# Second expert layer: the second group's scatters and the returns of finished tiles go out in pairs, each pair after the preceding pair has landed

## The reference, cut to what matters

```python
xf = x.reshape(-1, D)
logits = xf @ Wr.T + br
expert_idx = jnp.argmax(logits, axis=-1)               # one expert of 8 per token
h = relu(einsum('td,efd->etf', xf, W1) + b1[:, None, :])
y = einsum('etf,edf->etd', h, W2) + b2[:, None, :]
out = y[expert_idx, arange(tokens)]
x = _layernorm(x + out)
```

## Time and profile before

| what | number |
|---|---|
| runs, median (lowest, highest) | 1368.16 us (1364.99, 1369.56) |
| profiled execution, span | 1397.4 us |
| PE busy in the span | 1272.1 us (91%) |
| DVE busy | 1097.7 us (79%) |
| POOL busy | 1013.4 us (73%) |
| ACT busy | 947.2 us (68%) |
| chain that ended last | PE 49%, ACT 21%, DVE 16%, issue 8%, another core or an unknown queue 2% |
| L2079, 46 returns | 44.8 us busy, 974 ns each on average |
| L1972, 32 scatters of the second layer | 958 ns each (median) |

### The profile page before, as it was taken

The page is one execution under the profiler, slowest core; times in us unless marked ns, Lnnn a source line. Parts: engine busy times, 40 slices in busy tenths (PEclk is TensorE's granted clock), DMA queues, the critical chain, the costliest instruction groups (busy, mean ns, idle before and its releaser), DMA issues.

```text
span 1397.4 us, 27753 instructions
## 1 busy us (share of the span) xinstructions
PE 1272.1 (91%) x9894; PEld 962.1 (69%) x9894; DVE 1097.7 (79%) x1829; ACT 947.2 (68%) x1630; POOL 1013.4 (73%) x620
## 2 busy tenths in 40 slices
PE   6799999999999999999998779999989999986695
PEld 2567767676777676766766646689966666656693
DVE  5799999999999999999999953333357888874475
ACT  5888988898889888988988842245545555532243
POOL 2789999999999999999999916223334665664442
PEclk9999999999999999999999999999999999998798
DMA  5545434543444454444444351312152000021223
GB/s 187 145 131 161 138 139 118 161 149 129 139 139 165 133 150 139 164 132 152 139 146 111 114 216 47 90 44 86 56 157 86 2 1 1 13 64 34 79 72 100
DMA packets 153014, 154.73 MB, mean 111 GB/s; under 512 B 96624, under 2 KB 121712, under 8 KB 143168
## 3 DMA queue, kind: packets, MB, share of 16 engines
q1 hardware_dynamic: 148112, 143.16, 32.8%
q0 software_dynamic: 4768, 9.81, 2.2%
HBM read 138.66 MB, written 20.20 MB: 114 GB/s over the span
## 4 chain that ended last, share of the span: by engine, by line
PE 49%; ACT 21%; DVE 16%; issue 8%; another core or an unknown queue 2%; DMA 2%; POOL 1%; SPq 1%; DVEq 1%; POOLq 0%; ACTq 0%
DVE hh L887 7%; PE pq L410 6%; ACT da L720 6%; PE pa L506 4%; PE py L525 3%; ACT pa L725 3%; PE bank L1562 3%; PE bank L1558 2%; PE pr L2016 2%; PE bank L1572 2%; PE pr L2219 2%; PE pr L2030 2%; PE bank L1478 2%; DVE hh L897 2%
## 5 line engine op out<-in xcount | busy, mean ns | idle before, releaser
L1042 POOL TENSOR_TENSOR hc<-hh,cs 128x1024 f32<-128x1024 f32 x256 | 596.9, 2369 | 24.6 <-DVE hh L887 21.7
L887 DVE TENSOR_TENSOR_SCAN hh<-da,st,pa 128x512 f32<-128x512 f32 x240 | 292.7, 1261 | 14.1 <-PE pa L506 12.6
L525 PE MATMUL py<-ident,hc 128*128 128x128 f32 x2048 | 268.4, 277 | 7.4 <-ACT yt L738 5.8
L525 PEld LDWEIGHTS py<-ident,hc 128*128 128x128 f32 x2048 | 229.1, 141 | 54.4 <-issue 29.1
L506 PEld LDWEIGHTS pa<-dg,dtut 64*128 64x128 f32 x2560 | 160.9, 189 | 107.0 <-issue 103.2
L506 PE MATMUL pa<-dg,dtut 64*128 64x128 f32 x2560 | 189.8, 285 | 29.6 <-DVE hh L887 20.6
L720 ACT ACTIVATE da<-dt,w 128x512 f32<-128x512 f32 x320 | 209.7, 711 | 0.2
L897 DVE TENSOR_TENSOR_SCAN hh<-pa,st,hh 128x512 f32<-128x512 f32 x144 | 175.2, 1265 | 6.1 <-POOL hh L1032 3.7
L725 ACT ACTIVATE pa<-dt,w 128x512 f32<-128x512 f32 x192 | 124.5, 680 | 35.2 <-DVE hh L887 20.8
L410 PE MATMUL pq<-xn,w 128*128 128x512 f32 x248 | 124.6, 627 | 3.6 <-ACT xn L755 3.6
L1032 POOL TENSOR_TENSOR hh<-dtu,bs 128x1024 f32<-128x1024 f32 x48 | 112.8, 2365 | 3.1 <-issue 1.9
(11 more groups left out here) (341 smaller groups left out, 2643.8 us busy)
## 6 DMA issues: line engine op xcount, KB each, us to landing
cs<-bcrows SPq DMA_DIRECT2D x64, 1024.0 KB, 4.9
dg<-blocks SPq DMA_DIRECT2D x80, 256.0 KB, 5.0
bs<-bcrows SPq DMA_DIRECT2D x48, 256.0 KB, 3.7
blocks<-bcrows SPq DMA_DIRECT2D x320, 1.0 KB, 3.2
xsorted<-in_pads SPq DMA_DIRECT2D x13, 387.0 KB, 5.7
rot<-in_rot SPq DMA_DIRECT2D x4, 1024.0 KB, 4.9
wx<-in_l_w SPq DMA_DIRECT2D x4, 1024.0 KB, 10.0
ysort<-ytoken SPq DMA_DIRECT2D x14, 256.0 KB
```

The costliest lines, as they stand in the source:

```text
L525: i = pe.matmul(py[:, h * CH + kt * P:h * CH + (kt + 1) * P], hc[s % HCS][:, h, t], ident[:, :], is_transpose=True, start=n == 0 and kt == ...
L887: v.tensor_tensor_scan(hh[(NS * m + nj) % HHS][:, h, :], da[q % DAS][:, :], inflows, 0.0 if first else st[:, m % 2, nj, h:h + 1], ALU.mult ...
L1042: g.tensor_tensor(hc[s % HCS][:, :, :], hh[s % HHS][:, :, :], cs[j % 2][:, s % CG, :].unsqueeze(1).broadcast_to([P, HF, CH]), ALU.mult).th ...
```

## The change

In place 1's scatters GpSimd waits before every second tile, instead of before tile 8 alone, until all scatters of the place issued so far have landed. In the returns GpSimd waits before the tiles 2, 4, ..., 22 of each place until all returns of that place issued so far have landed. Nothing else differs.

```diff
 def scatter_gpsimd(place, tiles):
     ...
     for i in tiles:
-        if place and i and i % 8 == 0:
+        if place and i and i % 2 == 0:
             g.wait_ge(s_scat1[place], scat0[place] + 16 * i)
 ...
 def return_gpsimd(j):
     if j % SG == 0:
         g.wait_ge(s_token, j // SG + 2)
     g.wait_ge(s_ys, J0 + j + 1)
+    if j % SG and j % SG % 2 == 0:
+        g.wait_ge(s_ret1[j // SG], ret0[j // SG] + 16 * (j % SG))
     g.indirect_dma_start(out=ytoken, ...).then_inc(s_ret1[j // SG], 16)
```

## The result

| | before | after |
|---|---|---|
| runs, median (lowest, highest) | 1368.86 us (1364.99, 1372.72) | 1416.16 us (1415.07, 1417.48) |
| ratio to before, 95% interval | | 1.0346 (1.0320 to 1.0373) |
| profiled execution, span | 1397.4 us, a second one 1364.4 us | 1413.6 us |

The change costs 47.3 us. It was forecast as slower, at 1404 us in a range up to 1411; the direction and the mechanism held, the size did not.

A forecast was written before the change was run, and what follows sets the result against it. VectorE's row of finished tiles bounded the kernel; with the waits GpSimd's steps would. Without the profiled loss the last return moves from 1351.4 to 1387.5 us, and 1368.2 + 36.1 gives 1404 us, range 1374 to 1411.

The forecast's parts named there:

- The baseline: Profiled span without its loss is 1369.1 us, near the runs' 1368.2; the last return before the change starts at 1351.4.
- the 28.3 us: Time lost between tiles 6 and 33 on VectorE in the profiled execution, taken to be absent from the timed runs.
- Rival B: Timed runs have the same 28 us loss, so only 7.8 us are added: 1376 us; chance 0.18.
- C: Unknown releaser is GpSimd's own transfer traffic in every run, and pairs end it: not slower, 1362 us; chance 0.07.
- D: Waits are mostly met already, since tiles come 3.79 us a pair: no change, 1368 us; chance 0.05.
- The mechanism: GpSimd's 61 paced scatter and return steps become the bound; every tile is done before its return's turn.
- the tail: From the start of the last return to the end: 17.7 us, unchanged.
- the late sorted tiles: SyncE's load of place 1's sorted tiles goes from 1291.23 to about 1300 us, costing nothing in the end.
- the hold: VectorE, at about 1323.5 us, waits 24 us for place 0's tokens until 1347.6; tile 45 is finished at about 1374.
- The scatters: Place 1's scatters on GpSimd: 7 of 15 steps are boundaries, putting the last scatter at 1297.6 us, 8.7 us later.
- The price of one wait among the returns: Each of 22 boundaries among GpSimd's returns takes 2.71 us start to start, between 2.23 and 3.15, instead of 1.262.

The follow-up runs named there:

- the scatters alone: Changed kernel with only place 1's scatters in pairs, the returns running free as before: 1378.13 us, ratio 1.0074.
- the first experiment: The kernel before, unedited, profiled a second time: span 1364.4 us; its table sets first scatter, first return, last return and end against the changed kernel.
- returns alone: Changed kernel with only the returns in pairs, the scatters waiting once, at tile 8: 1408.07 us, ratio 1.0288.
- place 0 alone: Changed kernel with only place 0's returns in pairs, scatters as before: 1392.52 us, ratio 1.0163.
- the short load: Changed kernel with the load of place 0's tokens bringing one tile of each piece of four: one run, 1414.24 us.
- the waits turned: Changed kernel with the two waits ahead of a return in the other order, landing first, then finished tile: 1409.73 us, ratio 1.0286.
- two pairs in flight: Kernel before with returns in pairs, each waiting for the pair before the preceding one, a semaphore each for even and odd pairs: 1374.71 us, ratio 1.0047.
- the fours: Changed kernel with scatters as before and returns in fours, each begun once the preceding four has landed: 1388.16 us, ratio 1.0140.

## Why the prediction was wrong, step by step

**The baseline, right.** The step that took the 28.3 us out of the profiled execution put the last return 82.95 us after the first scatter (1351.4 less 1268.45); the second profile has 83.4. Rival B (the loss in every run, 1376 us) is thereby out. So is C: in the second profile GpSimd's transfers follow each other just as closely, and nobody waits for an unknown releaser. D is out by GpSimd's timeline, where it stands idle for 2 us or more ahead of each of the 22 boundaries. The second profiled execution ran like the timed ones, so the 27.8 us named under B were that one execution's, and not the price of being profiled.

**The mechanism, right.** GpSimd's own steps set the end; the tail is 17.8 us; VectorE is held for place 0's tokens, and tile 45 is done well before its return's turn. In the changed kernel the late sorted tiles cost nothing, as said; with the scatters alone they are the cost. That VectorE is held for 22.96 us where 24 was worked out is luck. Both ends of the hold came later than worked out: VectorE got there 10.0 us later (65.0 us after the first scatter instead of 55.1), after TensorE had stood 6.2 us for the sorted tiles, and the tokens 8.8 us later (88.0 instead of 79.2), because the returns took longer.

**The scatters, right.** Worked out at 30.45 us from first scatter to first return, measured 29.75.

**The price of one wait among the returns, wrong.** The step took 2.71 us from a scatter's row, between ends of 2.23 and 3.15, for each of 22 boundaries: 59.6 us. Measured, 17 of them take 2.96 to 2.98 and five take 4.75 to 5.23, together 75.4 us or 3.43 on average, which is above the upper end. That is 15.8 us, more than the 12 by which 1404 fell short of 1416; the scatters' 0.7 us less, and what stands below the table of the first experiment, go the other way. Of the 15.8, 5.7 are the 0.26 us by which an ordinary boundary is dearer than 2.71 (22 x 0.26): a return has two waits where the scatter has one, and the order of the two is worth 0.48 by itself. The other 10.1 are the five long ones. The row of 3.15 in the earlier trace rows said already that a landing doesn't always take the same time; it was taken as an upper end for the mean, when the stretch of the returns has a load of sorted tiles, a load of tokens and pieces of code beside them, and the scatters have none of the loads. In the kernel before no return of this layer has such a wait, so its price came from a neighbour, and the upper end did not leave room for that.

The fit in the Trainium skill's page "DMA: Bandwidth & Descriptors", section "Anatomy of one DMA — SWDGE (gpsimd) path", gives as an estimate 2.15 us for such a tile and agrees with the landing of an undisturbed return here (2.21 to 2.24 us). With other traffic beside it the landing took 4.0 to 4.3 us, and there the measurement decides.

## What to carry to other kernels

A wait for a landing between small transfers makes each boundary as long as the landing and the start of the next transfer together (here 2.2 and 0.7 us, instead of an issue step of 1.26); let the landing lie beside the next transfers' issue (two groups in flight, a semaphore for each) or leave the wait out. Price it from a row with the same waits and the same traffic beside it, and allow for the slowest landing of the stretch. Before a stall in one profiled execution is taken as the kernel's, set its span against the timed runs.

## What the runs showed of the hardware that had not been expected

- The order of two waits ahead of an indirect DMA is worth 0.48 us: 2.97 us from start to start with the late one as the second of the two, 2.49 with it as the first.
- A 64 KB indirect transfer that lands in 2.2 us alone took 4.0 us beside a 1 MB load and 4.3 us with one piece of code under way (`q8` brings 81 in the run, 1.33 MB in all, so some 16 KB each). The load was tested, the code only seen beside it.
- The boundary at tile 10 took 5.1 us in four kernels with pairs in place 0 (the changed kernel, returns alone, place 0 alone, the short load), 3.7 with the waits turned and 3.9 with two pairs in flight, 1.77 in the fours, where tile 10 waits for no landing, and 1.26 in the kernel before, although the landing took 2.2 us. In the four kernels with 5.1 us a piece of code is fetched on the queue `q14` near its end; with 3.7 and 3.9 us none stands in the stretch. That GpSimd waited for its own code there is a guess; it was not tried.
